# Target scores of the edge attention as three bf16 parts, with the one-hots of the lanes in bf16

## What is computed

```python
h_all = einsum('nf,rof->rno', x, W)                    # one row for each node and edge type
scores = (h_all[type, src] * attn_src).sum(-1) \
       + (h_all[type, dst] * attn_dst).sum(-1)         # (edges, 8); the second term: "target scores"
scores = where(scores > 0, scores, 0.2 * scores)
amax = maximum(segment_max(scores, dst), 0)
w = exp(scores - amax[dst])
out = segment_sum(h_all[type, src] * w[..., None], dst) / segment_sum(w, dst)
```

## Time and profile before

| | |
|---|---|
| median of 3 timed runs | 4262.99 us (4262.08 to 4263.6) |
| profiled execution, its own time | 4303.09 us |
| its span from first to last instruction | 4301.4 us |
| mean granted TensorE clock | 0.846 |
| TensorE matmuls busy | 3272.8 us (76%) |
| TensorE weight loads busy (beside matmuls) | 2416.5 us (56%) |
| VectorE busy | 2092.9 us (49%) |
| GpSimd busy | 1123.9 us (26%) |
| ScalarE busy | 772.1 us (18%) |

### The profile page before, as it was taken

One profiled execution on the slowest core, in us unless ns is written; L12 is line 12 of the kernel. 1 busy time (PEld: TensorE's weight loads), 2 busy tenths in 40 slices (PEclk: granted clock), 3 DMA queues, 4 the chain that ended last, 5 costly groups with the idle time before them and its releaser, 6 DMA issues. The chain is left out here.

```text
span 4301.4 us, 49813 instructions
## 1 busy us (share of the span) xinstructions
PE 3272.8 (76%) x14155; PEld 2416.5 (56%) x14156; DVE 2092.9 (49%) x4998; ACT 772.1 (18%) x1519; POOL 1123.9 (26%) x1178
## 2 busy tenths in 40 slices
PE   3899799979986245999819964676767677669998
PEld 2677588868865233888714534454545455545555
DVE  7999823323323640000046634666665766653333
ACT  0222122222222111332202310000000000022222
POOL 4810000000000224000040034666666666400000
PEclk9999999989998656999959976677777777769999
DMA  2722255444400014212124223444434344210000
GB/s 77 269 110 95 103 131 133 107 129 126 128 9 0 0 44 127 73 55 81 47 59 120 115 92 101 113 121 111 120 108 120 107 122 120 79 58 8 8 15 30
DMA packets 306806, 383.82 MB, mean 89 GB/s; under 512 B 40199, under 2 KB 249840, under 8 KB 303248
## 3 DMA queue, kind: packets, MB, share of 16 engines
q1 hardware_dynamic: 240016, 218.38, 16.3%
q0 software_dynamic: 50992, 146.13, 12.1%
q10 hardware_dynamic: 15696, 18.09, 1.3%
HBM read 270.97 MB, written 111.53 MB: 89 GB/s over the span
## 5 line engine op out<-in xcount | busy, mean ns | idle before, releaser
L2218 POOL DMA_INDIRECT relations_or_ring<-relation_rows,table_row x280 | 275.4, 983 | 468.7 <-SPq L1992 300.0
L496 PE MATMUL counts_acc<-onehot_lo,onehot_key 128*128 128x400 bf16 x2000 | 361.6, 336 | 46.7 <-DVE onehot_key L478 46.7
L475 DVE TENSOR_SCALAR onehot_lo<-node_ids,source_lo 128x800 bf16<-128x800 int16 x1000 | 360.2, 471 | 0.0
L496 PEld LDWEIGHTS counts_acc<-onehot_lo,onehot_key 128*128 128x128 bf16 x2000 | 267.9, 139 | 144.6 <-DVE onehot_key L478 86.4
L2358 PE MATMUL att_po<-att_near,att_onehotT 128*128 128x64 f32 x1568 | 240.7, 307 | 78.8 <-issue 72.6
L709 PE MATMUL agg_agg<-xn_or_ring,agg_slab 128*128 128x257 f32 x1250 | 278.5, 382 | 25.7 <-DMA agg_slab<-edge_counts 25.7
L709 PE MATMUL agg_agg<-x_gnn,agg_slab 128*128 128x257 f32 x1250 | 277.3, 381 | 19.1 <-DMA agg_slab<-edge_counts 19.1
L2218 POOL DMA_INDIRECT tables_or_ring<-relation_rows,table_row x252 | 250.4, 994 | 153.4 <-issue 71.3
L2218 POOL DMA_INDIRECT xn_or_ring<-relation_rows,table_row x252 | 250.4, 994 | 124.0 <-issue 71.3
L2358 PEld LDWEIGHTS att_po<-att_near,att_onehotT 128*128 128x128 f32 x1568 | 224.7, 222 | 88.0 <-issue 86.9
L709 PEld LDWEIGHTS agg_agg<-xn_or_ring,agg_slab 128*128 128x128 f32 x1250 | 238.5, 191 | 61.6 <-DMA agg_slab<-edge_counts 25.8
(11 more groups left out here) (430 smaller groups left out, 5355.3 us busy)
## 6 DMA issues: line engine op xcount, KB each, us to landing
agg_slab<-edge_counts SPq DMA_DIRECT2D x50, 1600.0 KB, 7.9
edge_counts<-counts_out SPq DMA_DIRECT2D x100, 400.0 KB, 2.3
relation_rows<-tables_or_ring SPq DMA_DIRECT2D x25, 1056.0 KB, 3.9
att_targets<-targets SPq DMA_DIRECT2D x28, 896.0 KB
wide_w<-L_ffn_W ACTq DMA_DIRECT2D x14, 1024.0 KB
expert_rows_in<-blank_rows POOLq DMA_DIRECT2D x34, 256.0 KB
expert_rows_out<-blank_rows POOLq DMA_DIRECT2D x33, 256.0 KB
ffn_xin<-expert_rows_in SPq DMA_DIRECT2D x31, 256.0 KB, 2.9
```

What stands on the lines that cost most here:

```text
L475: nc.vector.tensor_scalar(oh_lo[:, k, j, :], c.nodes[:, 0:LO], lo[:, ds(at + j, 1)], None, ALU.is_equal)
L496: mm = nc.tensor.matmul(acc[:, k, h, 0:HALF_LO], oh_key[:, k, :, j], oh_lo[:, k, j, h * HALF_LO:(h + 1) * HALF_LO], start=False, stop=Fals ...
L2218: self.nc.gpsimd.indirect_dma_start(self.slots[p % RING][:, j, :], None, self.rows_of, bass.IndirectOffsetOnAxis(ap=self.c.row[:, n:n + 1] ...
```

## The change

Target scores are kept as three bf16 numbers whose sum is the float32 number. In the tables' loop VectorE makes them (`split`): round to bf16, subtract, round the rest, subtract again. `split(t - 1)` stands between `moments(t)` and `scale(t)`, and `split(24)` behind the loop. The store of the target scores waits for it, and a row of them has 384 bytes, before 256. In the parts' loop the one-hots are bf16, `att_near` holds the three parts, and each chunk has three bf16 matmuls that add up in PSUM, before one float32 matmul. `late_scores` adds the three parts up first.

```diff
@@ mixing_tables
-    beyond, at = cut(at, sc)
+    rest, at = cut(at, sc)
...
+        parts = g.sb(ctx, f"{name}_near_parts", [P, 2, 3, sc], BF16)
+        beyond = g.sb(ctx, f"{name}_beyond", [P, 3 * sc], BF16)
...
+                def split(t):
+                    b = t % 2
+                    part = chain(v, split_s, 3 * t)
+                    v.wait_ge(read, (t + 1) * banks)
+                    if t >= 2:
+                        v.wait_ge(stored[b], 32 * (t // 2))
+                    part(nc.vector.tensor_copy(parts[:, b, 0, :], near[:, b, :]))
+                    part(nc.vector.tensor_tensor(rest, near[:, b, :], parts[:, b, 0, :], ALU.subtract))
+                    part(nc.vector.tensor_copy(parts[:, b, 1, :], rest))
+                    nc.vector.tensor_tensor(parts[:, b, 2, :], rest, parts[:, b, 1, :], ALU.subtract).then_inc(near_split, 1)
+                    v.wait_ge(near_split, t + 1)
...
                     moments(t)
+                    if t:
+                        split(t - 1)
...
                     scale(t)
+                split(NT - 1)
...
-                    sp.dma_start(dst_rows[t * P:(t + 1) * P, :], near[:, b, :]).then_inc(stored[b], 16)
+                    sp.wait_ge(near_split, t + 1)
+                    sp.dma_start(dst_rows[t * P:(t + 1) * P, :], parts[:, b, :, :].rearrange("p k n -> p (k n)")
+                                 ).then_inc(stored[b], 16)
@@ attend
-        ohT = g.sb(ctx, f"{name}_onehotT", [P, PE_LEN])
-        near = g.sb(ctx, f"{name}_near", [P, 2, sc])
+        ohT = g.sb(ctx, f"{name}_onehotT", [P, PE_LEN], BF16)
+        near = g.sb(ctx, f"{name}_near", [P, 2, 3, sc], BF16)
...
-                            mm = nc.tensor.matmul(po[:, j // bank, j % bank * sc:(j % bank + 1) * sc],
-                                                  ohT[:, j * P:(j + 1) * P], near[:, p % 2, :], start=True, stop=True)
+                            for k in range(3):
+                                mm = nc.tensor.matmul(po[:, j // bank, j % bank * sc:(j % bank + 1) * sc],
+                                                      ohT[:, j * P:(j + 1) * P], near[:, p % 2, k, :],
+                                                      start=(k == 0), stop=(k == 2))
@@ build_program
-    dst_rows = nc.dram_tensor("target_scores", (NP + P, R * HD), F32, kind="Internal").ap()
+    dst_rows = nc.dram_tensor("target_scores", (NP + P, 3 * R * HD), BF16, kind="Internal").ap()
```

More of the change, by code:

```diff
@@ L1820, in mixing_tables @@
         gaps.early(g, ctx)
+        parts = g.sb(ctx, f"{name}_near_parts", [P, 2, 3, sc], BF16)
+        beyond = g.sb(ctx, f"{name}_beyond", [P, 3 * sc], BF16)
+        split_s, near_split = g.sem(f"{name}_split_chain"), g.sem(f"{name}_near_split")
         pt = g.ps(ctx, f"{name}_pt", [P, MMN])
@@ L2299, in part_loads @@
                         sp.wait_ge(own_sum, p - 1)
[L2300 removed]
+                    sp.dma_start(near[:, p % 2, :, :].rearrange("p k n -> p (k n)"), near_rows[ds(at[p], P), :]).then_inc(near_in[p % 2], 16)
                 part_loads(0)
@@ L2760, in late_scores @@
         near = g.sb(ctx, "late_score_near", [P, R * HD])
+        near_parts = g.sb(ctx, "late_score_near_parts", [P, 3 * R * HD], BF16)
         of_type = g.sb(ctx, "late_score_type", [P, R])
@@ L2783, in _ @@
                         nc.gpsimd.indirect_dma_start(
-                            near, None, near_rows, bass.IndirectOffsetOnAxis(ap=near_ix[:, 0:1], axis=0)
+                            near_parts, None, near_rows, bass.IndirectOffsetOnAxis(ap=near_ix[:, 0:1], axis=0)
                         ).then_inc(landed, 16)
@@ L2794, in _ @@
                                                 ).then_inc(linked, 1)
-                        v.wait_ge(linked, n * 4 + 1)
+                        v.wait_ge(linked, n * 6 + 1)
+                        wide = R * HD
+                        nc.vector.tensor_tensor(near, near_parts[:, 0:wide], near_parts[:, wide:2 * wide], ALU.add
+                                                ).then_inc(linked, 1)
+                        v.wait_ge(linked, n * 6 + 2)
+                        nc.vector.tensor_tensor(near, near, near_parts[:, 2 * wide:3 * wide], ALU.add).then_inc(linked, 1)
+                        v.wait_ge(linked, n * 6 + 3)
                         by_head = near.rearrange("p (h r) -> p h r", h=HD)
@@ L2798, in _ @@
                                                 .to_broadcast([P, HD, R]), ALU.mult).then_inc(linked, 1)
-                        v.wait_ge(linked, n * 4 + 2)
+                        v.wait_ge(linked, n * 6 + 4)
                         nc.vector.tensor_reduce(own, by_head, AX, ALU.add).then_inc(linked, 1)
-                        v.wait_ge(linked, n * 4 + 3)
+                        v.wait_ge(linked, n * 6 + 5)
                         nc.vector.tensor_tensor(own, own, got[:, D:RW], ALU.add).then_inc(linked, 1)
-                        v.wait_ge(linked, n * 4 + 4)
+                        v.wait_ge(linked, n * 6 + 6)
                         nc.vector.scalar_tensor_tensor(
```

## The result

The changed kernel takes 4311.18 us (median of 4, 4308.71 to 4330.32) beside 4263.3 us for the kernel before on the same chip: ratio 1.0121, 95% interval 1.0091 to 1.0151. It is slower by 48 us where 45 us less were forecast. The profiled execution took 4330.32 us, span 4328.6.

A forecast was written before the change was run, and what follows sets the result against it. The prediction took TensorE to bound the tables' loop, and no full engine but a slow stretch of TensorE the parts' loop. Savings of 46 us less 1 us for the final split gave 45 us less: 4218 us, range 4140 to 4310.

The forecast's parts named there:

- the slow stretch: Parts' loop: some 14 us in which TensorE gets through about 20 instructions, costing 8 us an iteration or more.
- its lower bound, 0.028 and 0.056: Price of an own_scores bf16 pair, warm and cold; the groups would then save 4.6 us, 125 us in all: 4138.
- the second rival: In own_scores, small pairs are fed more slowly, above 0.073 us each; at 0.09 the kernel takes 4302; chance 0.12.
- The one-hots: Parts' loop, VectorE: each of two operations a part takes 1.0 us instead of 1.155; 0.15 us saved on the path.
- `split` is hidden: Tables' loop: four operations of 0.23 us, about 1.0 us a tile, fit in 2.05 us of slack and cost nothing.
- 1.1 + 0.15: Ahead of flip_back: groups 0 to 2 of own_scores save 1.1 us, the first half of the one-hots 0.15 us.
- 0.45: Behind flip_back: groups 3 to 6 of own_scores save 0.9 us, of which half is counted.
- 1.1 + 0.45 + 0.15 = 1.7 us, times 27: Parts' loop: saving an iteration from own_scores groups and one-hots, over 27 iterations with own_scores: 46 us.
- the slow stretch catches `flip_back`: Parts' loop: added loads and matmuls bring the stretch nearer flip_back, 20 iterations change kind: +46 us, 4309; chance 0.15.
- Its condition: The stretch catches flip_back's signal once it begins within some 2.5 us behind flip_back.

The follow-up runs named there:

- the first pair of traces: Profiled executions of the kernel before and the unaltered changed kernel for the first result: 4303.09 and 4330.32 us.
- the second: Traces of the unaltered changed kernel and the kernel before on another chip with stretches; measured 4351.4 us (ratio 1.0115) and 4295.89 us.
- all groups at `flip`: Changed kernel with all seven own_scores groups right behind flip, ahead of messages 0, and VectorE's second half of the one-hots moved too: 4364.32 us, ratio 1.0237.
- the last two experiments: Changed kernel with all seven own_scores groups ahead of messages 0, ratio 1.0237; with groups 0 to 2 behind flip and 3 to 6 behind messages 0, ratio 1.0063.
- three variants run once each: Changed kernel, chip without stretches: one product per chunk 4044.64 us; two products 4040.87; only 128 targets loaded from part 1 on 4042.9.
- the held gathers: Changed kernel with GpSimd holding a part's gathers from the thirteenth on until own_sum is signalled: 4285.85 us, ratio 1.0053.
- the groups behind messages 0: Changed kernel with own_scores groups 0 to 2 behind flip and 3 to 6 behind messages 0, VectorE's work moved likewise: 4289.19 us, ratio 1.0063.

## Why the prediction was wrong

**What bounds the kernel** was read rightly: no busy engine, but the slow stretch and the signals held in it.

**The sizes.** Small pairs come every 0.029 us at a granted clock of 1.00 (48 in 1.56 us, the last 0.2 of it its own) and every 0.053 at 0.50 (24 in 1.46 us behind the stretch of the changed kernel, 39 in 2.24 us with all groups at `flip`). The prediction took 0.055 for the fast clock and 0.11 for the slow one, twice too much at both; its lower bound, 0.028 and 0.056, was right. That also settles the second rival, that small pairs don't come that fast. The Trainium skill's page "TensorE: Matmul & The Clock Gate", section "Back-to-back issue gap", gives about 81 ns a matmul for a stream of load and matmul pairs with 128 moving columns. No run here has such a stream in bf16; the pairs here have 64 moving columns and come every 29 ns, so that figure is no guide to them. The one-hots take 0.69 us, not 1.0. `split` is hidden, as forecast: its operations take 0.18 to 0.23 us, and the part alone isn't slower. Without stretches an iteration is 2.4 us shorter, where the sum had 1.7, and the terms are distributed otherwise: ahead of `flip_back` 2.4 us were saved where the sum had 1.1 + 0.15, and behind it nothing where the sum had 0.45. The groups there end 2.1 us sooner, but VectorE's own work sets the time from `flip_back` to `flip`.

**The step that failed** is "an iteration is then shorter by 1.1 + 0.45 + 0.15 = 1.7 us, times 27": it prices the 28 added pairs by their duration alone, and lets everything behind the groups move forward as if the signals followed their matmuls. In place of 1.7 us less, an iteration took 0.9 us more in the first pair of traces and 1.9 us more in the second, by signals held back at `to_row`, `to_column` and `flip_back`. On a chip with stretches the number of pairs counts. In the order of pairs a part: 28 give 0.995 (one run), 56 give 0.988, 84 give 1.012 of the kernel before; and 28 empty pairs in the kernel before, with its float32 work untouched, give 1.020. 56 against 84 is a difference of 2.4%, while the 28 pairs between them are worth 0.8 us of TensorE's time in 41. With a quarter of the gathers the changed kernel is the faster one. Duration alone explains none of that. Number alone doesn't either: from 28 to 56 the time doesn't rise, and the variants with 84 pairs lie between 1.005 and 1.027, by where the pairs and the gathers stand.

**The rival that came nearest** is "the slow stretch catches `flip_back`". Its direction was right, and so was its idea that more loads and matmuls bring a held signal to a place where it costs more. Its place was right in 9 of 25 iterations of the first trace, where it had all 25, and in 2 of the second; in many of the others `to_row` or `to_column` is held for up to 9 us, a place that the prediction did not have. Its condition doesn't hold: with two products the stretch mostly begins less than 2.5 us behind `flip_back` too, and the signal isn't caught. So its 4309 us beside the 4311 measured are luck. The argument that gave it only 0.15 was weak: that the stretch stands at nearly the same distance behind `flip_back` looked like time. Counted from the gathers' resumption, about 160 to 175 loads and matmuls lie ahead of most stretches of the kernel before, 12 to 15 us; in the changed kernel's steady iterations it is about 145 to 150, 10 to 12 us. Time and count look the same as long as the list isn't changed, and neither stays the same when it is.

**What stays open.** The count is no law: it runs from about 100 (in the first `own_scores` of all) to 260, and the last two experiments were forecast by it the wrong way round. That the slow stretches and the loss need the gathers is shown (a quarter of them: no stretch, and the change saves 2.4 us an iteration; a pause put in by hand: the end of the stretch follows it). Whether it is GpSimd's issuing of the gathers or the transfers themselves, no run separates. What in the chip queues the signals, why the list slows to one instruction per 0.70 us, and why one chip of five shows none of it, no run here tells. Instruction packets alone don't bring the stretch (25 of them without one, above); whether a packet comes late while gathers run was not tested by itself. The forecast for a chip without stretches would have had the right sign but not the size: 0.5%, in three variants run once each, with GpSimd as the bound at 35 us.

No exact variant of the changed kernel beat the kernel before where the stretches are; the best of them were the held gathers and the groups behind messages 0.

## What to carry to other kernels

An engine that stops for "issue" while its inputs are there, and signals that arrive in one bundle long after their matmuls, are one symptom: look at what GpSimd's gathers do at that time, above all at when they pause. There, count instructions as well as their time: three cheap matmuls in place of two dear ones can lose. Read the waits of every signal in such a loop, and in more than one trace: here the same loss of 1.2% sat mainly at one signal in one trace and at another in the next. Before a trade of that kind, take the suspected partner away in a trial (here the gathers) to see which chain is being shortened, and give a wait that already costs 12 us in some iterations more than a small chance of spreading.

## What the runs showed of the hardware

- TensorE's slow stretch: one instruction, or a few together, per 0.70 us or a multiple of it (one iteration of the changed kernel: 3513.22, 3513.92, 3515.32, 3516.02), mostly for 9 to 20 us, ending mostly 2 to 5 us after the start of the last gather of a run; none in the loop with 7 gathers a part instead of 28.
- Signals of finished matmuls up to 12.7 us late under gathers, in an iteration without a slow stretch.
- A bf16 pair of 128x128 load and 64 columns every 0.029 us over 48 pairs at a granted clock of 1.00; every 0.053 at 0.50 (39 in 2.24 us). The float32 pair: 0.11 us at 1.00 (32 in 3.70 us).
- Chip to chip 4064, 4263 and 4300 us for one kernel, the first without stretches: a comparison across chips would have hidden a change of 1%.
